# Two multi-head attentions on Trainium2: scores that stay in PSUM, with maxima per group and exponents per head

## What is computed

```python
q = proj(query, Wq, SQ)            # query = layernorm(x), 256 rows in each of 8 batches
k = proj(key, Wk, SKV)             # 77 keys in each batch
v = proj(value, Wv, SKV)
scores = jnp.einsum('bhqd,bhkd->bhqk', q, k) / np.sqrt(HEAD_DIM)
scores = scores + attention_bias[:, None, None, :]
probs = jax.nn.softmax(scores, axis=-1)
out = jnp.einsum('bhqk,bhkd->bhqd', probs, v)
...
x = x + jnp.tanh(g_xattn[1]) * (out @ Wo.T)
```

## Time and profile before

| | |
|---|---|
| median of 3 runs | 1342.4 us (1341.94 to 1349.6) |
| profiled execution | 1342.16 us |
| its span in the profile | 1340.5 us |
| mean granted TensorE clock | 0.867 of full speed |

### The profile page before, as it was taken

One profiled execution on the slowest core, in us unless ns is written; L12 is line 12 of the kernel. 1 busy time (PEld: TensorE's weight loads), 2 busy tenths in 40 slices (PEclk: granted clock), 3 DMA queues, 4 the chain that ended last, 5 costly groups with the idle time before them and its releaser, 6 DMA issues. The chain is left out here.

```text
span 1340.5 us, 26537 instructions
## 1 busy us (share of the span) xinstructions
PE 1036.2 (77%) x8492; PEld 771.8 (58%) x8493; DVE 800.2 (60%) x1767; ACT 554.9 (41%) x1319; POOL 578.3 (43%) x738
## 2 busy tenths in 40 slices
PE   5778287886558999940999916799987879997998
PEld 3666167784335777730899802455555557776443
DVE  4576163443383789865555544346663648886876
ACT  2452023342124666634343315556651257773000
POOL 1473703555344777634000062546662257772000
PEclk9986588998678999855999956889998979996999
DMA  3463208883113111147777421000001000000000
GB/s 110 117 178 122 102 3 289 293 296 119 54 32 114 48 36 36 48 168 283 250 254 253 168 70 53 1 1 1 1 1 47 2 12 17 16 18 6 16 23 24
DMA packets 70682, 123.47 MB, mean 92 GB/s; under 512 B 15481, under 2 KB 41859, under 8 KB 70595
## 3 DMA queue, kind: packets, MB, share of 16 engines
q1 hardware_dynamic: 63011, 101.64, 22.8%
q0 software_dynamic: 7584, 20.72, 4.6%
HBM read 52.98 MB, written 24.64 MB: 58 GB/s over the span
## 5 line engine op out<-in xcount | busy, mean ns | idle before, releaser
L2472 PE MATMUL bank<-l0f_x_high,l_weights 128*128 128x256 bf16 x256 | 51.0, 316 | 33.4 <-issue 20.2
L2881 POOL DMA_DIRECT2D l_results<-keep x23 | 12.5, 544 | 135.6 <-DVE keep L2984 129.7
L303 ACT ACTIVATE xnT<-bank 128x256 f32<-128x256 f32 (+1 forms) x112 | 41.3, 380 | 70.1 <-PE bank L292 69.3
L3256 PE MATMUL bank<-l_weights,room 128*128 x552 | 65.1, 273 | 4.3 <-DVE room L3284 2.9
L3244 PE MATMUL bank<-room,xnT 128*128 128x128 bf16 x1104 | 67.6, 223 | 0.0
L3244 PEld LDWEIGHTS bank<-room,xnT 128*128 128x128 bf16 x1104 | 65.8, 100 | 0.3
L2304 DVE SCALAR_TENSOR_TENSOR l3f_total<-bank,l3f_share,l3f_total 128x256 f32<-128x256 f32 x112 | 54.2, 484 | 15.6 <-PE bank L2222 12.0
L1849 POOL TENSOR_TENSOR l2x_probs<-l2x_probs,l2x_inverse 128x333 f32<-128x333 f32 x64 | 49.1, 789 | 29.0 <-DVE l2x_inverse L1755 29.0
L2687 PE MATMUL bank<-room,l0r_placed 128*128 128x128 bf16 x936 | 61.3, 224 | 0.0
L3256 PEld LDWEIGHTS bank<-l_weights,room 128*128 128x128 bf16 x552 | 52.7, 98 | 12.4 <-issue 5.4
L2687 PEld LDWEIGHTS bank<-room,l0r_placed 128*128 128x128 bf16 x936 | 58.2, 101 | 0.6
(11 more groups left out here) (437 smaller groups left out, 3162.5 us busy)
## 6 DMA issues: line engine op xcount, KB each, us to landing
xnT<-l_weights SPq DMA_DIRECT2D x23, 1024.0 KB, 5.1
l0r_placed<-l_weights SPq DMA_DIRECT2D x39, 512.0 KB, 3.6
l0w_staging<-in_L_ffn_weights SPq DMA_DIRECT2D x16, 480.0 KB, 3.8
l_weights<-in_L_ffn_weights SPq DMA_DIRECT2D x16, 384.0 KB, 3.1
room<-in_L_ffn_weights SPq DMA_DIRECT2D x12, 512.0 KB
room<-l_rows SPq DMA_DIRECT2D x39, 128.0 KB, 3.2
l_results<-room POOLq DMA_DIRECT2D x39, 128.0 KB, 3.1
xnT<-in_L_ffn_weights SPq DMA_DIRECT2D x8, 512.0 KB, 7.9
```

The costliest lines, as they stand in the source:

```text
L303: act.activation(self.chip.xnT[:, :, span(t, P)], bank[:, 0:DIM].rearrange("p (k n) -> p k n", k=KD), ACT.Copy).then_inc(self.copied, 1)
L2472: last = pe.matmul(self.bank[:, c, branch * width:(branch + 1) * width], self.weights[w][:, at:at + P], x[:, s, k, :], start=(i == 1), sto ...
L3256: last = pe.matmul(bank[:, 2 + u, 0:DIM], h[:, u, c * P:(c + 1) * P], expert_part(split[:, w, :, :], e, KD * hidden_width + c * DIM, DIM), ...
```

## The change

Scores are no longer copied to SBUF. DVE takes the negated maxima of a group straight from its PSUM bank, as soon as the group is there. ACT makes the exponents from the same bank, one instruction for each head (16 a tile in place of one), with the head's negated maximum as the bias. POOL's subtraction goes. The factor 1/4 on the scores moves from the exponent's scale into the constant `head_of`, so the key bias of layer 1 is no longer multiplied by 4 ahead of it. A bank of scores is now free when its four exponents are done, not when it was copied. The scores run one tile ahead instead of two, the queries are projected in the tile u = 0 for the next batch, and PE, ACT and DVE go group by group. POOL does the next norm's power first. The eight logits in the last batch stand in one piece, ahead of the last attend.

```diff
             def scores(b, u, slot, groups=range(GROUPS)):
...
                 for g in groups:
-                    wait(pe, scores_copied, GROUPS * t + g - 1)
+                    wait(pe, probs_ready, GROUPS * t + g - 1)
...
             def transpose_probs(t, u, g):
+                pe.wait_ge(probs_ready, GROUPS * t + g + 1)
                 wait(pe, low_copied, GROUPS * t + g - 1)
...
-                    pe.wait_ge(probs_ready, t + 1)
-                    for half in range(2):
-                        groups = (2 * half, 2 * half + 1)
-                        for g in groups:
-                            transpose_probs(t, u, g)
-                        if half == 1 and not first:
+                    for g in range(GROUPS):
+                        transpose_probs(t, u, g)
+                        if u == 0:
+                            scores(b, 1, b % 2, (g,))
+                        elif ahead >= 1:
+                            scores(b + 1, 0, (b + 1) % 2, (g,))
+                        if g == 1 and not first:
+                            transpose_mixed(t - 1)
+                        if g == 2 and not first:
                             project_out(t - 1)
-                        if ahead >= 1:
-                            scores(b + 1, u, (b + 1) % 2, groups)
-                        else:
-                            pe.wait_ge(scores_copied, GROUPS * TILES)
-                            chip.logits.some(pe, 2, norm)
-                        if half == 0 and not first:
-                            transpose_mixed(t - 1)
-                    if u == 1 and ahead >= 2:
-                        project_q(b + 2)
+                    if u == 0 and ahead >= 1:
+                        project_q(b + 1)
+                    if u == 1 and ahead == 0:
+                        chip.logits.some(pe, 8, norm)
...
-            def exponents(t, u):
-                act.wait_ge(shifted, t + 1)
-                act.activation(probs[:, u, :], probs[:, u, :], ACT.Exp,
-                               scale=HEAD ** -0.5).then_inc(probs_ready, 1)
+            def exponents(t, u, g):
+                act.wait_ge(max_ready, GROUPS * t + g + 1)
+                for h in range(GROUP):
+                    n = g * GROUP + h
+                    last = act.activation(probs[:, u, n * KEYS:(n + 1) * KEYS], s_bank[g % 2][:, h * KEYS:(h + 1) * KEYS],
+                                          ACT.Exp, bias=neg_max[:, u, n:n + 1])
+                last.then_inc(probs_ready, 1)
...
+                    high_probsT(t, 0)
+                    high_probsT(t, 1)
+                    if not is_step(t, 0):
+                        copy_mixedT(t - 1)
+                    for g in range(GROUPS):
+                        if ahead >= 1 or u == 0:
+                            exponents(t + 1, 1 - u, g)
+                        if g + 2 < GROUPS:
+                            high_probsT(t, g + 2)
+                    if u == 0 and ahead >= 1:
+                        copy_q(b + 1)
                     feed.high(act, b, u)
...
-            def maxima(t, u):
-                wait(dve, shifted, t - 1)
-                dve.wait_ge(scores_copied, GROUPS * t + GROUPS)
-                dve.tensor_reduce(row_max[:, u, :], raw[:, u, :].rearrange("p (h k) -> p h k", h=HEADS),
-                                  AX_X, ALU.max).then_inc(max_ready, 1)
+            def maxima(t, u, g):
+                dve.wait_ge(scores_ready, GROUPS * t + g + 1)
+                dve.tensor_reduce(neg_max[:, u, g * GROUP:(g + 1) * GROUP],
+                                  s_bank[g % 2][:, 0:width].rearrange("p (h k) -> p h k", h=GROUP),
+                                  AX_X, ALU.max, negate=True).then_inc(max_ready, 1)
...
+                    for g in range(GROUPS):
+                        low_probsT(t, g)
+                        if ahead >= 1 or u == 0:
+                            maxima(t + 1, 1 - u, g)
```

More of the change, by code:

```diff
@@ L731 @@
 GROUPS = HEADS // GROUP
-BIAS_STEPS = 9
 class HeadsAhead(Loads):
@@ L805, in vector_bias @@
         chain(dve.memset(rows[:, :], 0.0))
-        chain(dve.tensor_scalar(bias, bias, HEAD ** 0.5, None, ALU.mult))
         chain(dve.tensor_copy(high[:, :], bias))
@@ L877, in multi_head_attention @@
         v_placed = st.sem("v_placed")
-        raw = st.sb("scores", [P, TPB, HEADS * KEYS])
         probs = st.sb("probs", [P, TPB, HEADS * KEYS])
         probsT = [st.sb(f"probsT_{n}", [KEYS, HEADS * P], BF16) for n in ("high", "low")]
-        row_max = st.sb("row_max", [P, TPB, HEADS])
+        neg_max = st.sb("neg_max", [P, TPB, HEADS])
         inverse = st.sb("inverse", [P, HEADS])
@@ L900, in multi_head_attention @@
         scores_ready = st.sem("scores_ready")
-        scores_copied = st.sem("scores_copied")
         max_ready = st.sem("max_ready")
-        shifted = st.sem("shifted")
         probs_ready = st.sem("probs_ready")
@@ L1003, in _ @@
                 pe.wait_ge(bias_ones_ready, 1)
-            for u in range(TPB):
-                scores(0, u, 0)
-            project_q(1)
+            scores(0, 0, 0)
             project_v(late)
@@ L1075, in copy_mixedT @@
                                ACT.Copy).then_inc(mixedT_ready, 1)
[L1077 to L1080, removed]
+            for g in range(GROUPS):
+                exponents(0, 0, g)
             if len(late):
@@ L1161, in _ @@
             copy_v(early)
-            for u in range(TPB):
-                maxima(u, u)
+            for g in range(GROUPS):
+                maxima(0, 0, g)
             copy_v(late)
@@ L1208, in spread_keys @@
                                        ALU.mult).then_inc(k_diag_ready, 1)
[L1210 to L1213, removed]
-                                   raw[:, u, :].rearrange("p (h k) -> p h k", h=HEADS), row_max[:, u, :].unsqueeze(2).to_broadcast([P, HEADS, KEYS]),
-                                   ALU.subtract).then_inc(shifted, 1)
             def place_values(b):
@@ L1222, in _ @@
             spread_keys(0, 0)
-            for u in range(TPB):
-                shift(u, u)
             spread_keys(1, 1)
@@ L1230, in batch @@
                     t = TPB * b + u
+                    if not is_step(b, 0):
+                        norm.gpsimd(pool, t - 2, u)
                     if u == 0:
                         place_values(b)
+                    elif ahead >= 2:
+                        spread_keys(b + 2, b % 2)
                     if not key_bias:
                         pool.tensor_tensor(nth(chip.x, t), nth(chip.x, t), bo[:, :], ALU.add).then_inc(x_biased, 1)
-                    if not is_step(t, 0) and (ahead >= 1 or u == 0):
-                        shift(t + 1, 1 - u)
-                    if not is_step(t, 0):
-                        norm.gpsimd(pool, t - 1, 1 - u)
-                    if u == 0 and ahead >= 2:
-                        spread_keys(b + 2, b % 2)
                     feed.low(pool, b, u)
             batches(pool, batch)
-            norm.gpsimd(pool, TILES - 1, 1)
+            for u in range(TPB):
+                norm.gpsimd(pool, TILES - TPB + u, u)
 L2_HEADS, L2_HEAD = 4, 64
@@ L3388, in lay_out @@
     a["key_bias"] = inputs["fside_BxS2_0"].reshape(CTX)
-    a["head_of"] = np.kron(np.eye(CHUNK_HEADS, dtype=np.float32), np.ones((HEAD, 1), np.float32))
+    a["head_of"] = np.kron(np.eye(CHUNK_HEADS, dtype=np.float32), np.full((HEAD, 1), HEAD ** -0.5, np.float32))
     a["L3_xattn_Wq"], a["L3_xattn_Wo"] = inputs["L3_xattn_Wq"], inputs["L3_xattn_Wp"]
```

## The result

The changed kernel takes 1358.59 us (median of 4 runs, 1356.61 to 1360.1) against 1344.34 for the kernel before on the same chip (4 runs, 1341.94 to 1349.6): ratio 1.010, 95% interval 1.0064 to 1.0135. It is slower, by about 1%. The forecast was 1349, with 1324 to 1366 around it.

A forecast was written before the change was run, and what follows sets the result against it. PE's own work, with a bank wait replacing POOL's ring, was taken to bound the stages. Span 1340.5 + 8.6 (layer 3) - 1.9 (layer 1) = 1347.2, + 1.66 = 1348.9, forecast 1349 us, range 1324 to 1366.

The forecast's parts named there:

- E0: ACT's exponents of the first group, whose end frees the bank for the third scores; predicted PE idle 1.2 us per tile.
- The walk: Predicted schedule of one tile on PE, ACT and DVE: two tiles 17.63 us in layer 3, 19.01 in layer 1.
- S2: PE's scores of the third group, predicted to start at 3.85 us in layer 3, after 1.2 us of idle.
- E: Time on ACT until a group's last exponent is written, taken as 0.98 us, at 0.22 an exponent.
- X: DVE's maxima of 128x308 from PSUM, four a tile, taken as 0.47 us, or 0.40 in a full queue.
- the ring: Layer 3's chain of maxima, POOL's subtraction (2.25 us), exponents, transposes and split copies; predicted to give way to a bank wait.
- the first rival: PE not kept waiting for the bank: 1322 us, or 1335 with half the wait; chance 0.20, including more than foreseen.
- The last tiles: Time added for the final tile of each attention stage: 8.6 us in layer 3, 8.1 in layer 1.
- The heads: Stretch up to a stage's first normalise, predicted 0.5 us earlier in layer 3 and 0.6 in layer 1.
- The clock: Rival: PE's granted clock falls after idling in mid-tile, once a pair in both stages: 1363 us; chance 0.14.
- ACT did not become the bound: Rival that ACT becomes the bound at 0.326 us an exponent: 1361 us, deciding from 0.27; chance 0.13.
- POOL did not hold A back: Rival that POOL's queue delays the norm scaling on DVE, +0.5 us a tile: 1364 us; chance 0.05.

The follow-up runs named there:

- the control: The changed kernel measured again with no edit: 1357.2 us, ratio 1.011 against the kernel before.
- bias alone: Against the kernel before: POOL's subtraction gone, 16 exponents with bias on ACT from scores in SBUF, old order and banks kept: 1435.58 us, ratio 1.0705.
- that one edit: Against the changed kernel: a third PSUM bank for scores, groups in banks 0, 1, 7, 1: 1278.04 us, ratio 0.9886 to the kernel before.
- the same swap: First exponents moved ahead of the mixed copy in ACT's queue: changed kernel, 1297.74 us, ratio 1.003; three-bank kernel with groups in 0, 1, 7, 0, 1336.95 us, 0.9954.
- the second map: Against the kernel with three score banks: groups in banks 0, 1, 7, 0 instead of 0, 1, 7, 1: 1324.46 us, ratio 0.9858 to the kernel before.
- the logits in two pieces: Against the changed kernel: the last batch's eight logits in two pieces of four, behind the last tile's second and fourth transposes: 1306.65 us, ratio 1.0093.

## Why the prediction was right or wrong

**Right: the mechanism.** The third scores wait for E0 in every tile (forecast 1.2, measured 0.76 to 1.03). The walk of a tile u = 1 of layer 3 put S2 at 3.85, O at 4.37, T3 at 5.24, S3 at 5.71 and Nt at 8.02 after T0; the trace has 3.72, 4.34, 5.21, 5.64 and 7.92. E was 0.98 and is 0.97, X 0.47 and is 0.465. POOL is off the ring. The direction was the likelier of the two sides named outright (slower 0.32, faster 0.18), but half of the chance stood on "within 1%", and the ratio lies at that bound. The size was not right: the forecast had +6.7 us of span and the trace has +16.7, and for layer 1 the forecast had the wrong sign (-1.9 with its head, measured +2.8).

**Right: the price of the first rival.** PE not kept waiting was to give 15.9 for two tiles and 1322 in all; with the bank wait taken away it is 16.1 and 1324.5 (and 17.1 for two tiles of layer 1, where it had 17.0). The prediction's sum for it has a slip: 7 x 15.9, less 1.15, plus 8.6 is 118.8 and not 117.7, so its own terms give 1323. It was no forecast of this change, since the wait was there.

**Wrong: sizes, together 10.0 us of span (1357.2 against 1347.2).**

- The steps of layer 1: 7 x 19.01 - 1.75 = 131.3 up to the 15th normalise, measured 133.6 (567.1 less 433.5): +2.3. Two tiles take 19.3 in the hardware loop.
- The steps of layer 3: 122.3, measured 123.1: +0.8. T0 of the next tile starts 0.57 after Nt at the turns of the hardware loop (1162.83 to 1163.40, and once more in the stage), and 0.27 elsewhere, where the walk had 0.22.
- The last tiles, "8.6" and "8.1": measured 9.96 and 9.95, +1.35 and +1.9. In both PE's clock is down for a part of the tile, and O takes nearly twice as long (1.91 and 1.83 for 1.03). Layer 3's is not fixed: the control has 8.12. The windows of the changed kernel and then of the control show it; why the clock fell in the one and not in the other is not shown, since PE had waited 0.60 in both just before:

```profile
1225.00:1230.00 5.00, 4.31 (x20) 3.27 (x19) 2.64 (x7) 2.22 (x6) 2.06 (x4) 0.66 0.00 0
```

```profile
1225.00:1230.00 5.00, 3.91 (x33) 3.23 (x30) 3.78 (x10) 3.52 (x11) 2.05 (x4) 1.00 0.00 0
```

- The heads, -0.5 and -0.6: measured +0.2 (first scores of layer 3 to its first normalise, 20.46 to 20.67) and -0.1, together +1.2. What the single tile of lead saved was given back in full.
- Outside both attentions nothing was forecast, and there are +2.7 between them and -0.3 behind. The first scores of layer 3 come 504.7 after the last normalise of layer 1 in place of 502.0. Every kernel with the changed order has 504.2 to 505.3 there, and bias alone, with the old order, 501.4, so it is no accident of one run. That code is unchanged. Most of it, 2.1 us, arises at the end of layer 2's attention, where PE's granted clock falls sooner. Its window and last output projection there, before and then after:

```profile
1020.00:1025.00 5.00, 3.37 (x24) 2.85 (x22) 2.53 (x8) 0.32 (x1) 1.59 (x4) 1.00 0.01 2
1020.92 1.10 PE L1452 MATMUL bank<-room,l2x_mixedT 128*128 128x256 f32 x4 [0.33 <-DVE x_res L1760]
...
1023.00:1028.00 5.00, 4.99 (x18) 4.20 (x16) 1.41 (x4) 0.38 (x1) 0.74 (x2) 0.50 0.00 0
1025.60 2.04 PE L1425 MATMUL bank<-room,l2x_mixedT 128*128 128x256 f32 x4
```

Why it falls sooner there stays open.

**The other rivals.** The clock did not fall in mid-stage, with 1.0 of waiting in every tile; it fell in the last tiles, after 1.5 of waiting in layer 1 and 0.6 in layer 3 (and not in the control, after the same 0.6). Two windows of the changed kernel, one in either stage (the clock is the number ahead of the last two):

```profile
510.00:520.00 10.00, 8.77 (x93) 6.78 (x91) 7.09 (x17) 7.86 (x25) 6.27 (x9) 1.00 0.14 41
...
1140.00:1150.00 10.00, 7.94 (x83) 6.25 (x84) 6.67 (x16) 8.09 (x30) 5.23 (x8) 1.00 0.06 15
```

So the stretches at 0.67 of the earlier trace rows went, as forecast, and layer 1 was slower all the same. ACT did not become the bound: the exponents start (0.97 - 0.33) / 3 = 0.21 apart. POOL did not hold A back: A takes 400 ns at best, 402 in the median and at most 899 now, against up to 2477.

**The exponents from SBUF and from PSUM.** From SBUF, 16 of them take 4.09, so (4.09 - 0.35) / 15 = 0.25 apart; from PSUM 0.21. The first agrees with the Trainium skill, "ScalarE: Activation LUTs" (What ACT_TABLE_LOAD costs), by whose figures for an ACTIVATE with a bias pointer an estimate is 0.25; the second is lower. "Perfetto Trace Analysis" (Optimizing Scalar/DVE Operations) of the Trainium skill gives ScalarE an access overhead of about 93 ns on SBUF and 51 on PSUM; that would make the difference, 0.04, and these runs agree with it.

**Not separated:** whether the group-wise order or the reading from PSUM makes the exponents per head affordable. The kernel with bias alone lacks both.

## What to carry to other kernels

When a consumer reads PSUM directly in place of a copy, the bank stays taken until the last consumer in the chain is done: walk the producer's queue up to the next use of that bank, and look for a spare bank before judging the fusion; here that one edit turned 1% slower into 1.1 to 1.4% faster, and which bank the fourth group took was worth another 0.2 to 0.4 us in every two tiles. An engine's instruction in a ring is worth only the time that the next engine in fact waits for it. The best order in a queue depends on which wait ends last: the same swap won 0.5 to 0.7% with two banks and lost 0.7 to 1.0% with three, so try it again after each such change.

## What the runs showed of the hardware that was not expected

- An exponent of 128x77 with a bias from SBUF takes 0.25 in a full queue when its source is SBUF and 0.21 when it is PSUM.
- After a wait of 3.11 us of PE at the turn of a tile the granted clock was 0.50 (1186 to 1190 us); after waits of 1.0, once in a tile, it stayed at 1.00. In the last tile of layer 3, after the same wait of 0.60, the same program ran once at 0.66 and once at 1.00 (1225 to 1230 us), so such a fall is not the program's alone. A fall, with the wait of 0.52 ahead of it, cost 1.3 us in one step with the second map, and one cost 1.8 in that last tile, as much as all that some of these edits win or lose in a stage: look at the granted clock before two stages are compared.
- The kernel before took 1294.8 in one set of runs and 1343.6 in another, with the attentions as long in both. The traces (the logits in two pieces in the first set, the control in the second) have the difference in two stretches of layer 0's feed-forward. At 139 to 174 us of the control, PE stands idle between matmuls in time for which the profile shows no releaser, and the stretch takes some 31 us longer; a second one, up to 361, takes some 23 longer. What it is stays open. Times don't compare from set to set; the lengths of the attention stages do.
